# Softmax chain across rows of edges: both directions in one visit to TensorE, in four iterations for six

## The reference

```python
scores = jnp.einsum('ed,d->e', gathered, W[0])                 # first layer, one head
seg_max = jax.ops.segment_max(scores, he_idx, num_segments=num_hyperedges)
w = jnp.exp(scores - seg_max[he_idx])
denom = jax.ops.segment_sum(w, he_idx, num_segments=num_hyperedges)
w_norm = w / jnp.maximum(denom, 1e-20)[he_idx]
out = jax.ops.segment_sum(w_norm[:, None] * gathered, he_idx, num_segments=num_hyperedges)
...
e = jax.nn.leaky_relu(s_src[src] + s_dst[dst], negative_slope=LEAKY_SLOPE)   # second layer, four heads
e_max = jax.ops.segment_max(e, dst, num_segments=N)
ex = jnp.exp(e - e_max[dst])
den = jax.ops.segment_sum(ex, dst, num_segments=N)
num = jax.ops.segment_sum(ex[:, :, None] * m, dst, num_segments=N)
```

## Time and profile before

| | us |
|---|---|
| three runs | 10307.41, 10285.1, 10297.61 |
| median | 10297.61 |
| profiled execution, its own time | 10333.18 |
| its span, first to last instruction | 10331.4 |
| mean granted TensorE clock | 0.675 |

### The profile page before, as it was taken

How to read it: one execution, slowest core, us unless ns; L and a number is a source line. 1 busy time by engine, 2 the same in 40 slices (tenths; PEclk the granted TensorE clock), 3 DMA queues, 4 the chain that set the end, 5 groups by cost and what they waited for, 6 DMA issues and landing times. The chain is left out here.

```text
span 10331.4 us, 125962 instructions
## 1 busy us (share of the span) xinstructions
PE 5216.4 (50%) x26943; PEld 4473.0 (43%) x27385; DVE 5156.8 (50%) x11738; ACT 2353.7 (23%) x7991; POOL 6140.1 (59%) x6653
## 2 busy tenths in 40 slices
PE   1544444447366555656673333333345655666655
PEld 1433333435355544545552232322235555555553
DVE  4644444546466666666651222222235555555556
ACT  1122212224244444444450000000012111111114
POOL 5666666662565666665515666666656666666664
PEclk9665555667677777777785566656666666666667
DMA  4222222222444444444321111111113333333331
GB/s 105 45 47 46 47 46 46 46 46 85 100 99 98 99 100 101 100 101 98 88 68 42 44 45 44 45 45 45 46 53 112 100 99 102 100 100 101 99 101 45
DMA packets 876674, 770.31 MB, mean 75 GB/s; under 512 B 388487, under 2 KB 735372, under 8 KB 875553
## 3 DMA queue, kind: packets, MB, share of 16 engines
q0 software_dynamic: 229424, 526.62, 20.1%
q1 hardware_dynamic: 630335, 229.55, 9.4%
q10 hardware_dynamic: 16184, 6.05, 0.3%
HBM read 707.25 MB, written 54.31 MB: 74 GB/s over the span
## 5 line engine op out<-in xcount | busy, mean ns | idle before, releaser
L590 POOL DMA_INDIRECT rows_sum<-t_d,idx x1532 | 1447.9, 945 | 1086.3 <-issue 432.3
L1024 POOL DMA_INDIRECT rows_h<-t_d,idx x1563 | 1485.2, 950 | 1008.4 <-issue 396.3
L590 POOL DMA_INDIRECT rows_mlp<-t_d,idx x1548 | 1469.2, 949 | 842.5 <-remote 426.4
L1024 POOL DMA_INDIRECT rows<-t_d,idx x1477 | 1399.7, 948 | 837.2 <-issue 407.3
L1169 PE MATMUL pn_h<-S_h,rows_h 128*128 128x128 f32 x6252 | 1129.0, 345 | 141.6 <-issue 114.3
L1169 PEld LDWEIGHTS pn_h<-S_h,rows_h 128*128 128x128 f32 x6252 | 1079.4, 257 | 278.7 <-issue 245.8
L787 DVE TENSOR_TENSOR big<-big,pn_sum 128x512 f32 x391 | 269.2, 688 | 1779.9 <-remote 1369.7
L1064 ACT ACTIVATE rows_h<-rows_h,wc_h 128x64 f32<-128x64 f32 x4688 | 1137.7, 334 | 25.3 <-issue 15.1
L635 PE MATMUL pre_mlp<-dw_mlp,ST_mlp 128*128 128x128 f32 x3126 | 673.8, 380 | 481.0 <-DVE ST_mlp L59 191.7
L635 PEld LDWEIGHTS pre_mlp<-dw_mlp,ST_mlp 128*128 128x128 f32 x3126 | 593.9, 282 | 528.2 <-issue 496.5
L655 PE MATMUL pn_mlp<-S_mlp,rows_mlp 128*128 128x128 f32 x3126 | 679.3, 390 | 195.9 <-DVE big L787 97.4
(11 more groups left out here) (363 smaller groups left out, 8663.2 us busy)
## 6 DMA issues: line engine op xcount, KB each, us to landing
dw_mlp<-bd_d SPq DMA_DIRECT2D x1563, 64.0 KB
frow_sum<-t_d SPq DMA_DIRECT2D x2048, 0.5 KB
frow_sum<-t_d ACTq DMA_DIRECT2D x1920, 0.5 KB
frow_mlp<-t_d ACTq DMA_DIRECT2D x1920, 0.5 KB
frow_h<-t_d SPq DMA_DIRECT2D x1792, 0.5 KB
lrb_h<-lrrow_d SPq DMA_DIRECT2D x196, 128.0 KB
lrb_mlp<-lrrow_d SPq DMA_DIRECT2D x98, 256.0 KB
rows_h<-t_d,idx POOLq DMA_INDIRECT x1563
```

What stands on the lines that cost most here:

```text
L590: e.indirect_dma_start(rows[:, g % NR, j, :], None, table, bass.IndirectOffsetOnAxis(ap=idx[:, b, t:t + 1].bitcast(I32), axis=0)).then_inc ...
L1024: e.indirect_dma_start(rows[:, g % NR, j, :], None, table, bass.IndirectOffsetOnAxis(ap=idx[:, b16, t:t + 1].bitcast(I32), axis=0)).then_i ...
```

## The change

CHAIN has 15 links for 23: the two scans of the rows give their ends together (`ends` for scan1 and scan2's first half; `sums` for sum1 and sum2), PE turns both columns of ends in one visit (`rp`, and `rp_back` in another part of the same bank), DVE does the forward and the backward scan over the line one behind the other, and PE turns both lines back in one visit into the two columns of `cp`. `col` has two columns, `line` is two lines (second stage alone), and the bound of the backward sum is a relu'd line `cap_back` that ACT makes in `caps`. For the sum, the backward line is scanned with additions before the row carries are known: so the row's backward carry gets the row's own forward end added (`col[:, 1:2] + f[:, P-1:P]`), and `alpha`'s divisor is the sum of both carries. The end of each line beyond the last tile is set by a memset each time. STEPS is 4 for 6: chain work stands in the last four iterations before a batch. AHEAD is GB + STEPS, 12 for 14 in the second stage. In ACT's and PE's lists `exps` moves from step 2 to 1, `weights` and the early placing from 5 to 3. The number of transpositions, ten a batch, and of scans stays.

```diff
@@ -823,8 +823,8 @@
         c["landed"][g % NR] += 16 * sum(4 * g + j not in FETCHED[1] + ([] if mlp else FETCHED[0]) for j in range(SIZE[g]))
 
 
-CHAIN = ("score", "scoreT", "scan1", "row1", "scanI", "col1", "scan2", "row2", "scanJ", "col2", "scan3", "exp",
-         "sum1", "row3", "scanT", "col3", "sum2", "row4", "scanK", "col4", "norm", "wT", "wc")
+CHAIN = ("score", "scoreT", "ends", "row1", "scanI", "col1", "most", "exp",
+         "sums", "row2", "scanT", "col2", "norm", "wT", "wc")
 
...
-    AHEAD = NR - 2
-    STEPS, ROOT, LEAN = 6, 28, 1 if gat else 0
+    STEPS, ROOT, LEAN = 4, 28, 1 if gat else 0
+    AHEAD = GB + STEPS
...
-        scT, rp, cp, ap = small[:, 0:P], small[0:1, P:2 * P], small[:, 2 * P:2 * P + 1], small[:, 2 * P + 8:2 * P + 8 + blocks]
+        scT, cp, ap = small[:, 0:P], small[:, 2 * P:2 * P + 2], small[:, 2 * P + 8:2 * P + 8 + blocks]
+        rp, rp_back = small[0:1, P:2 * P], small[0:1, 3 * P:4 * P]
...
-                e.activation(L.cap[:, :], row_pen(b)[:, 0, :, :].rearrange("o h k -> o (h k)"), ACT.Relu)
+                for k, t in enumerate((L.cap, L.cap_back)):
+                    e.activation(t[:, :], row_pen(b)[:, k, :, :].rearrange("o h k -> o (h k)"), ACT.Relu)
...
-            def turn(b, after, out, x):
+            def turn(b, after, *moves):
 
                 e.wait_ge(s_chain, at(b, after))
-                n = x.shape[0]
-                e.transpose(out, x, ident[0:n, 0:n]).then_inc(s_chain, 1)
+                for out, x in moves:
+                    n = x.shape[0]
+                    last = e.transpose(out, x, ident[0:n, 0:n])
+                last.then_inc(s_chain, 1)
+
+            def ends_to_rows(b, after):
+
+                n = count[b] * heads
+                turn(b, after, (rp[:, 0:n], f[0:n, P - 1:P]), (rp_back[:, 0:n], g1[0:n, 0:1]))
+
+            def rows_to_cols(b, after, ahead):
+
+                n = count[b] * heads
+                x = (ahead[:, 0:n], lines[b].J[:, 1:n + 1]) if not gat else (line[0][:, 0:n], line[1][:, 0:n])
+                turn(b, after, *((cp[0:n, k:k + 1], x[k]) for k in range(2)))
 
             def chain_mid(b, step):
-
-                n = count[b] * heads
-                entries = lines[b].I[:, 0:n] if not gat else line[:, 0:n]
-                later = lines[b].J[:, 1:n + 1] if not gat else line[:, 0:n]
-                if step == 0:
-                    turn(b, "score", scT[0:n, :], sc[:, :, :].rearrange("p t h -> p (t h)")[:, 0:n])
-                if step == 1:
-                    turn(b, "scanI", cp[0:n, :], entries)
-                if step == 2:
-                    turn(b, "scanJ", cp[0:n, :], later)
-                if step == 3:
-                    turn(b, "sum1", rp[:, 0:n], f[0:n, P - 1:P])
-                if step == 4:
-                    turn(b, "sum2", rp[:, 0:n], g1[0:n, 0:1])
-                if step == 5:
-                    turn(b, "norm", wp[:, b % 2, 0:n], wr[0:n, :])
-
-            def chain_end(b, step):
 
                 n = count[b] * heads
                 if step == 0:
-                    turn(b, "scan1", rp[:, 0:n], f[0:n, P - 1:P])
+                    turn(b, "score", (scT[0:n, :], sc[:, :, :].rearrange("p t h -> p (t h)")[:, 0:n]))
                 if step == 1:
-                    turn(b, "scan2", rp[:, 0:n], g1[0:n, 0:1])
+                    rows_to_cols(b, "scanI", lines[b].I)
+                if step == 2:
+                    ends_to_rows(b, "sums")
                 if step == 3:
-                    turn(b, "scanT", cp[0:n, :], lines[b].T[:, 0:n] if not gat else line[:, 0:n])
-                if step == 4:
-                    e.wait_ge(s_chain, at(b, "scanK"))
+                    turn(b, "norm", (wp[:, b % 2, 0:n], wr[0:n, :]))
+
+            def chain_end(b, step):
+
+                if step == 0:
+                    ends_to_rows(b, "ends")
+                if step == 2:
+                    e.wait_ge(s_chain, at(b, "scanT"))
                     if not gat:
                         e.matmul(ap, ones[0:1, :], al[:, :], start=True, stop=True)
                     else:
                         for k in range(2):
                             e.matmul(ap[k * DH:(k + 1) * DH, :], ones[0:1, 0:DH], al[:, k:heads:2], start=True, stop=True)
-                    turn(b, "scanK", cp[0:n, :], lines[b].J[:, 1:n + 1] if not gat else line[:, 0:n])
+                    rows_to_cols(b, "scanT", lines[b].T)
 
...
+            def from_row(L, x, i, n, row):
+                return e.tensor_copy(L.part(x, i, i + n), row[:, 0:n * heads].rearrange("o (t h) -> o h t", h=heads))
+
+            def to_lines(L, x, n):
+
+                e.drain()
+                e.tensor_copy(line[0][:, 0:n * heads].rearrange("o (t h) -> o h t", h=heads), L.part(x, 0, n))
+                return e.tensor_copy(line[1][:, 0:n * heads].rearrange("o (t h) -> o h t", h=heads), L.part(L.J, 1, n + 1))
...
-                    from_row(L, L.R, 1, n)
-                    e.drain()
-                    last = forward(L, L.I, L.R, row_pen(b)[:, 0, :, :].rearrange("o h k -> o (h k)"), -BIG, ALU.max)
-                    to_line(L, L.I, 0, n, last).then_inc(s_chain, 1)
+                    from_row(L, L.R, 1, n, rp)
+                    e.memset(L.part(L.RB, n, n + 1), -BIG)
+                    from_row(L, L.RB, 0, n, rp_back)
+                    e.drain()
+                    backward(L, L.RB, flat(row_pen(b)[:, 1, :, :]), -BIG, ALU.max)
+                    forward(L, L.I, L.R, flat(row_pen(b)[:, 0, :, :]), -BIG, ALU.max)
+                    e.drain()
+                    e.tensor_tensor(al[:, :], flat(L.part(L.R, 0, 1)), flat(L.part(L.J, 0, 1)), ALU.subtract)
+                    e.drain()
+                    last = e.tensor_scalar(al[:, :], al[:, :], 0.0, None, ALU.min)
+                    if gat:
+                        last = to_lines(L, L.I, n)
+                    last.then_inc(s_chain, 1)
                 if step == 2:
-                    e.wait_ge(s_chain, at(b, "row2"))
-                    from_row(L, L.RB, 0, n)
-                    e.drain()
-                    backward(L, b, L.J, L.RB)
-                    e.drain()
-                    e.tensor_tensor(al[:, :], L.part(L.R, 0, 1).rearrange("o h k -> o (h k)"),
-                                    L.part(L.J, 0, 1).rearrange("o h k -> o (h k)"), ALU.subtract)
-                    e.drain()
-                    last = e.tensor_scalar(al[:, :], al[:, :], 0.0, None, ALU.min)
-                    to_line(L, L.J, 1, n, last).then_inc(s_chain, 1)
+                    e.wait_ge(s_chain, at(b, "exp"))
+                    e.tensor_tensor_scan(f[0:m, :], cap[0:m, 0:P], wr[0:m, :], 0.0, ALU.min, ALU.add)
+                    e.drain()
+                    scan_back(b, g1, f, -BIG).then_inc(s_chain, 1)
                 if step == 3:
-                    e.wait_ge(s_chain, at(b, "exp"))
-                    e.tensor_tensor_scan(f[0:m, :], cap[0:m, 0:P], wr[0:m, :], 0.0, ALU.min, ALU.add).then_inc(s_chain, 1)
-                if step == 4:
-                    e.wait_ge(s_chain, at(b, "col3"))
-                    e.tensor_copy(col[0:m, :], cp[0:m, :])
-                    e.drain()
-                    e.tensor_tensor_scan(f[0:m, :], cap[0:m, 0:P], wr[0:m, :], col[0:m, 0:1], ALU.min, ALU.add)
-                    e.drain()
-                    scan_back(b, g1, f, -BIG).then_inc(s_chain, 1)
-                if step == 5:
-                    e.wait_ge(s_chain, at(b, "col4"))
+                    e.wait_ge(s_chain, at(b, "col2"))
                     e.tensor_copy(col[0:m, :], cp[0:m, :])
                     e.tensor_copy(alpha[:, :], ap)
                     e.drain()
-                    scan_back(b, g1, f, col[0:m, 0:1])
+                    e.tensor_tensor_scan(f[0:m, :], cap[0:m, 0:P], wr[0:m, :], col[0:m, 0:1], ALU.min, ALU.add)
+                    e.drain()
+                    e.tensor_tensor(col[0:m, 1:2], col[0:m, 1:2], f[0:m, P - 1:P], ALU.add)
+                    e.drain()
+                    scan_back(b, g1, f, col[0:m, 1:2])
                     e.drain()
...
-                    e.tensor_tensor_scan(f[0:m, :], pen[0:m, b % 2, 0:P], scT[0:m, :], -BIG, ALU.min, ALU.max
-                                         ).then_inc(s_chain, 1)
+                    e.tensor_tensor_scan(f[0:m, :], pen[0:m, b % 2, 0:P], scT[0:m, :], -BIG, ALU.min, ALU.max)
+                    e.drain()
+                    scan_back(b, g1, f, -BIG).then_inc(s_chain, 1)
                 if step == 1:
                     e.wait_ge(s_chain, at(b, "col1"))
                     e.tensor_copy(col[0:m, :], cp[0:m, :])
                     e.drain()
                     e.tensor_tensor_scan(f[0:m, :], pen[0:m, b % 2, 0:P], scT[0:m, :], col[0:m, 0:1], ALU.min, ALU.max)
                     e.drain()
-                    scan_back(b, g1, f, -BIG).then_inc(s_chain, 1)
+                    scan_back(b, g1, f, col[0:m, 1:2])
+                    e.drain()
```

(43 more changed lines are left out.)

33 lines of the change are left out of this document (14 added, 19 removed).

## The result

The changed kernel takes **10388.67 us** (median of 6 runs, 10381.81 to 10398.06), the kernel before 10302.51 (10276.5 to 10320.71) beside it: ratio **1.0086**, 95% interval 1.0069 to 1.0102. I had forecast 10262, with 10145 to 10370 as the range. It is slower by 86 us, within rival 4's range and outside my own. The profiled executions are 10333.18 and 10382.58, 49 us apart; single executions scatter by some 20 us, so I take sizes from the traces only where they are larger. Here L1 is 72 us longer in the changed kernel's trace, and the two light stages, whose code is the same, are together 28 us shorter, which hides a part of it. (The ratios are those on record; the quotient of two medians differs from them by up to 0.0006.)

A forecast was written before the change was run, and what follows sets the result against it. No engine always busy; POOL's gathers pace it, with PE's signals held until POOL pauses. DVE's work -12, visits -43, packing +20 sum to -35 us from 10297.6: 10262 us, range 10145 to 10370.

The forecast's parts named there:

- rival 4: L1 steps 1 and 2: packed iterations outlast four gathers, so slower, 10335 to 10415 us; chance 0.24.
- the packing's term: L1, same chain work in four iterations: two too long by 0.3 and 0.1 us, 0.4 us x 48, +20 us.
- if visits fall on a hold as before: L1 packed iterations: POOL's pause also comes later by DVE's extra work, up to 2.7 us a batch, +130 us.
- The visits, -43: Both softmax stages: joined PE visits save DVE waits before col2 and row4, -43 us, ends 0 and -156.
- the fifth: Share of DVE's waits before exposed visits in L1 and L0 (169 and 50 us) taken as saved, -43 us.
- DVE's work, -12: L1 and L0 batches: fewer drains against small added operations, net -0.2 us a batch, -12 us, ends 0 and -20.
- the 5.9 us of step 3: L1's last chain iteration, with the 0.95 us reciprocal: forecast VectorE length 5.9 us, below four gathers' 6.3.
- L0, priced at 0: First softmax stage: packing costs 0, since its plain part is shorter and POOL has 32 slots.
- RB_h under 40: Sign of being right: L1's DVE idle time before RB_h falls from 148 us to under 40.
- case 4's signs: Slower outcome's signs: gather over 1.60 us, POOL idle behind PE above 610 us, DVE's idle in chain iterations grown.
- Col1 over 100: Sign of being right: L1's DVE idle time before col_h at L1351's place stays over 100 us or grows.
- the hold might depend on how many signals are waited for: What would make the forecast all wrong: fewer visits would then be worth more than any term.

The follow-up runs named there:

- six iterations: The changed kernel's joined visits spread over six iterations for four (AHEAD 14), against the kernel before: 1.0000 on chip 4; 10139.24 us, 0.9959 on chip 11.
- free pads: Kernel before plus 128x128 reciprocals behind L1's chain work: steps 2 and 5 1.0003, 0.9997; steps 4 and 5 1.0012, steps 2 to 5 1.0009 with held signals.
- six even: Joined visits over six iterations, sums in 2, scanT in 3, norm's forward scan and addition in 4, against the kernel before: 10226.93 us, 0.9913 on chip 1.
- the spread version with full iterations: The changed kernel's same steps put in iterations 0, 1, 3, 5 of six, against the kernel before: 0.9949 on chip 1.

## Why the prediction was wrong

**The step that failed** is the packing's term, +20 us. The prediction had a price for "if visits fall on a hold as before", up to +130; it gave this to rival 4 and took +20 without a reason for the one over the other. On chip 11 going from six iterations to four costs 134 us (10139.24 to 10273.07): 87 in L1 and 39, priced at nothing, in L0. The step behind it is that two iterations would be too long by 0.3 and 0.1 us and the other time would hide, with the visits' gain as a term beside it. But with row work joined, a hold at scoreT has 2.2 us for 1.2 of chain work between the release and the group's second half, and the next hand-over stands in the very next iteration. In the sum these were two terms of opposite sign, each sized by itself; in the kernel one undoes the other. L1 alone came out at +51 to +72 us for my -35 in all.

**The visits, -43.** The waits at RB_h and at L1358, 169 us in L1, did go, but in the changed kernel other waits came for them: DVE's "remote" idle time is 471 us before and 455 after in 2775:5137, 10.1 and 10.0 us a batch. With six iterations joining does gain, 36 us, near the 43 that I had taken. That is luck in part: the fifth (of 219 us, L0 included) had no row behind it. One reading beside it was too strong: plain iterations don't lose "as much" at L1480, for of its 210.9 us 128 lie in them. And the visits were ten for six, not eleven, since `alpha` shared col4's.

**DVE's work, -12**: nothing. Without place 0, where DVE waits for PE, the shortest intervals of a batch's iterations add up to 32.8 us for 32.8 (32.8 for 32.9 on chip 11). (The prediction had 36 us for a whole batch; it is 37.7 at the shortest, for one of the two plain iterations holds the rescaling and takes 4.9.) By the Trainium skill's rule (VectorE: DVE Perf Modes, Rules for kernel authors), which I had set against my term, it would have been +20; the traces bear out neither that nor my -12.

**Packing**: its lengths were right. I had 6.6, 6.4, 5.9 and 5.3 us, and the shortest are 6.66, 6.16, 6.05 and 5.17. The conclusion, 0.3 and 0.1 us above 6.3 and so 0.4 us a batch, compared lengths, and so did the price of up to 2.7 us. The free pads show that length isn't the measure: the place of the work is, ahead of a hand-over or behind it. Rival 4 had the sign, and its range (10335 to 10415) holds the result. But its mechanism as written, packed iterations that outlast four gathers, is what the free pads speak against; of it the part on visits that fall on a hold is left. That the result lies in its range is thus luck in part.

**Norm** I left within the 5.9 us of step 3, as cover for itself. It has 0.81 us more in front of `wT`, and behind it there are 8 us until the first group's slot. Over 49 batches that is 40 us at most, where place 0's excess grew by 71 and 33 in the two pairs of traces. I had moved the forward scan without asking who waits for the iteration's result. But the longer norm is not the cause by itself: the six iterations of chip 11 have the same norm (2.97 us), and place 0 has 66 us there for 53 before and 86 in the changed kernel. So up to 13 us can be norm's and the other 20 came with the packing. Between six and six even, where norm is the short one again, place 0 goes from 66 to 52, but these are on two chips and the even one differs in other steps too.

**L0, priced at 0**: 4.5 us in the first pair of traces, 33.6 on chip 11. On chip 11 six iterations take 2293 us there for 2299 before and 2332 changed, so it goes with the packing there; but each of these is one execution, and the first pair has a seventh of it. The excess wasn't worked out for it, and why 32 slots don't cover it stays open.

**The signs.** RB_h under 40: right. The gather over 1.60 and POOL's idle time behind PE above 610 (423.3 + 199.7 = 623) were case 4's signs, and came. Col1 over 100: wrong, 41.5; the hold moved one visit up, to L1349. Landing waits stayed at 0.0 on the first chip. DVE's busy time per batch is the same, and the full iterations without a hold take 5.2 to 6.7 us, as foretold. That the hold might depend on how many signals are waited for isn't borne out by the changed kernel (10.1 and 10.0 us of "remote" a batch); the six iterations' 8.3 leaves it open.

**What is shown and what is argued.** Shown: joining alone gains (0.9959), packing it loses (1.0090), spreading the very same iterations removes the loss (0.9949), work behind a hand-over is free and ahead of it costs (0.9997, 1.0043), and the loss goes with held signals (0.9990 without). Not separated: the number of iterations and AHEAD. Argued from the traces: that in a packed chain each late hand-over is handed on, as an iteration in between would take it up. Why place 0 has only 27 us of excess in the spread version with full iterations, with norm as long as in the changed kernel, I can't say, beyond that a row of eight gathers stands ahead of it in 43 of 45 batches, so its pause starts later.

## What to carry to other kernels

With held signals, fewer hand-overs are worth something only as long as the work is not also moved closer together: leave an iteration between a result and the step that uses it, and put the merged work there. For each piece that you move, ask what stands between it and the next group's release, not how long its iteration gets; the same 0.8 us were free behind the hand-over and cost 0.4% ahead of it. And look for the floor first: once the pace of the unloaded stages is known (1.48 us), only the places where a slot is later than that can be gained or lost.

## What was unexpected of the hardware

The same program took 8481 to 8497 us on two chips and 10175 to 10311 on four others: 1.25 us a gather for 1.47 to 1.64, though one gather lasts the same (947 to 955 ns on average in L1), and a 128x1024 accumulation too (1222 ns). On the faster ones no signal is held. What makes a chip one or the other no run here shows. Where a memset and a drain stand on GpSimd behind four gathers, the next gather starts 2.7 us and more after the last record of the four has ended. And the held time is not a fixed sum: per batch of L1 DVE's part of it went from 10.3 us to 6.5 as the same chain was spread out.
